# A VectorE loop over four pairs in place of eight, rings of four slots, and the edge mask made beside the scores

## The chip, the cores and the metric

The kernel runs on one core of a Trainium2 chip. Its engines are PE (TensorE), VectorE (DVE), ScalarE (ACT), GpSimd (POOL) and SyncE (SP), each with an instruction stream of its own; they meet by semaphores. The metric is the device time of one execution in microseconds (us), the median of several runs.

## The reference

Four graph layers over 6,250 nodes of 128 features and 200,000 edges follow one another, each on a normalised and rectified copy `h` of the nodes and each added to them: a sum over neighbours with two linear layers, a filter convolution, an attention layer (GATv2), and the relation layer. The change touches the last alone:

```python
def relation(entity_emb, rel_embed_weight, W, heads, rels, tails):
    e_h, e_t, e_r = entity_emb[heads], entity_emb[tails], rel_embed_weight[rels]
    score = jnp.sum(e_t * jnp.tanh(e_h + e_r), axis=-1)
    score_exp = jnp.exp(score - jnp.max(score))
    score_sum = segment_sum(score_exp, heads, n)
    attn = score_exp / (score_sum[heads] + 1e-10)
    agg = segment_sum(attn[:, None] * e_t, heads, n)
    return leaky_relu((entity_emb + agg) @ W.T, 0.2)
x = x + relation(h, rel, W, src, edge_type_64, dst)
```

## The kernel before

The layers run one after the other. For the relation layer the edges lie sorted by `src`, in groups of 512 (`GE`, four columns of 128 edges: `KG` = 4). Nodes lie in windows of 128. A *pair* is a group and a window that it has edges in; 392 groups are loaded and 440 pairs (`NG`) are worked through, in the order of lists that the chip has made itself (`k.plan`). An edge of the group that belongs to another window is a foreign edge of the pair.

A pair goes through these steps, all in `relation`:
- SyncE loads the group's records (`rows`, L2251); GpSimd gathers its 512 target rows with four indirect DMAs (`far`, L2278) into a ring of eight slots, and waits on `rows_free` for a free one (SyncE's L2265).
- `columns` (VectorE, L2297 to 2299): each edge's place in the window (`rel`), its type (`kind`), and the mask `hide`, a large negative number for foreign edges.
- `spread_keys` (PE, L2405) and `take_keys` (ScalarE, L2360) bring place and type into rows; `one_hots` (VectorE, L2306, L2307) compares them into `hot_t` and `kind_t`.
- `near` (PE, L2417 to 2420) fetches `e_h + e_r` with matmuls over these, `terms` (ScalarE, L2365) takes the tanh.
- `score_edges` (VectorE): four products with a sum (`work`, L2318), the mask added (`score`, L2324), the group's highest per partition (`peak`, L2327).
- `spreads` (PE, L2435), `running_max` (VectorE, L2334 `before`, L2336 `gmax`, L2339 `cur`), `exps` (ScalarE, L2371, L2373).
- `turn_hot` (PE, L2428), `share_out` (ScalarE, L2382), `sums` (PE, L2444), `add` (VectorE, L2347: the running row, `cur`), `keep` (ScalarE, L2391).

Each engine runs a hardware loop (`skewed`) whose body works through several pairs (`turn`) and holds the steps in the order of the call. A step with lead 7 (`COLS`) works seven pairs ahead of one with lead 0 (`ADD`), so in one pass of VectorE the add is for pair n, the scores for n+3, the one-hots for n+5, the columns for n+7. At the head of `columns` and of `score_edges` the engine reads the number of the pair's group from the lists into a register (`pair_group`, L1230); records and gathered rows are then addressed by it. VectorE's, ScalarE's and PE's loops here take eight pairs (`S` = 2 x `U` = 8); the loop's end is L1206. `wait(..., behind)` waits until a step is done for the pair that lies `behind` before, which guards a ring of that many slots.

Of the kernel before, what the change touches and what calls it, by code (L numbers as in the profile page):

```python
# [18 lines left out]
P = 128  # L19
# [2184 lines left out]
def relation(k):  # L2204
# [15 lines left out]
    with ExitStack() as own:  # L2220
        sb = lambda name, shape, dt=F32: k.sb(own, "r_" + name, shape, dt)
        rows, keys = sb("rows", [P, R, KG, MW - M_SRC], I32), sb("keys", [P, 2, 2, GE], BF16)
        rel, hide, kind = sb("rel", [P, S, KG]), sb("hide", [P, S, KG]), sb("kind", [P, S, KG])
        hot_t, kind_t = sb("hot_t", [P, H, GE], BF16), sb("kind_t", [P, U, GE], BF16)
        far = sb("far", [P, S, KG, XW])
        work, raw, score, peak = sb("work", [P, KG, D]), sb("raw", [P, KG]), sb("score", [P, S, KG]), sb("peak", [P, S])
        gmax, before, factor = sb("gmax", [P, 1]), sb("before", [P, S]), sb("factor", [P, S])
        prob, share = sb("prob", [P, S, KG]), k.store[:, 10 * NL:10 * NL + 2 * GE].rearrange("p (b q c) -> p b q c", b=2, q=KG)
# [15 lines left out]
        with nc.Block() as block:  # L2244
# [39 lines left out]
            @block.vector  # L2284
            def _(dve):
                now = Counts(dve)
                k.link(dve, nc.vector.memset(cur[:, :, :], 0.0))
                k.link(dve, nc.vector.memset(cur[:, :, D + 1:D + 2], -LOW))
                k.link(dve, nc.vector.memset(far[:, :, :, D:XW], 1.0))
                start(dve, cols_ready, onehotT_ready, edge_dot, masked, scores, group_max, exp_in, added)  # L2290

                def columns(g, a):
                    u, f = a % S, bass.ds(g + a, 1)
                    group = pair_group(dve, k, o, g + a)
                    dve.wait_ge(records_in, in_order(group))
                    row = lambda c: flat(rows[:, bass.ds(slot_of(group, R), 1), :, c - M_SRC])
                    nc.vector.tensor_scalar(rel[:, u, :], row(M_SRC), base[:, f], None, ALU.subtract)  # L2297
                    nc.vector.tensor_copy(kind[:, u, :], row(M_TYPE)).then_inc(cols_ready, 1)
                    nc.vector.tensor_scalar(hide[:, u, :], row(M_BASE), base[:, f], -BIG, ALU.not_equal, ALU.mult)

                def one_hots(g, a):
                    h, b = a % H, a % 2
                    wait(dve, now, keys_taken, g, a)
                    wait(dve, now, onehot_turned, g, a, H)
                    wait(dve, now, near_ready, g, a, U)
                    nc.vector.tensor_scalar(hot_t[:, h, :], keys[:, b, 0, :], k.part_id[:, 0:1], None, ALU.is_equal)  # L2306
                    nc.vector.tensor_scalar(kind_t[:, a % U, :], keys[:, b, 1, :], k.part_id[:, 1:2], None, ALU.is_equal)\  # L2307
                        .then_inc(onehotT_ready, 1)

                def score_edges(g, a):  # L2310
                    u, b = a % S, a % 2
                    group = pair_group(dve, k, o, g + a)
                    slot = bass.ds(slot_of(group), 1)
                    dve.wait_ge(rows_here, in_order(group))
                    wait(dve, now, edge_term, g, a)
                    wait(dve, now, scores, g, a, 1)
                    for q in range(KG):
                        last = nc.vector.scalar_tensor_tensor(  # L2318
                            work[:, q, :], near_ps[b][:, q * D:(q + 1) * D], 1.0, flat(far[:, slot, q, 0:D]), ALU.mult, ALU.mult,
                            accum_out=raw[:, q:q + 1])  # L2320
                    last.then_inc(edge_dot, 1)
                    wait(dve, now, edge_dot, g, a)
                    wait(dve, now, weighed, g, a, S)
                    nc.vector.tensor_tensor(score[:, u, :], raw[:, :], hide[:, u, :], ALU.add).then_inc(masked, 1)  # L2324
                    wait(dve, now, masked, g, a)
                    wait(dve, now, spread, g, a, S)
                    nc.vector.tensor_reduce(peak[:, u:u + 1], score[:, u, :], AX, ALU.max).then_inc(scores, 1)  # L2327

                def running_max(g, a):
                    u, f = a % S, bass.ds(g + a, 1)  # L2330
                    past = cur[:, (u - 1) % S, D + 1:D + 2]
                    wait(dve, now, exp_in, g, a, 1)
                    wait(dve, now, shrink, g, a, S)
# [3 lines left out]
                    wait(dve, now, kept, g, a, S)  # L2337
                    wait(dve, now, group_max, g, a)
                    nc.vector.scalar_tensor_tensor(cur[:, u, D + 1:D + 2], gmax[:, :], -1.0, past, ALU.mult, ALU.min)\  # L2339
                        .then_inc(exp_in, 1)  # L2340

                def add(g, a):
                    u, b = a % S, a % 2
# [3 lines left out]
                    nc.vector.scalar_tensor_tensor(cur[:, u, 0:D + 1], cur[:, (u - 1) % S, 0:D + 1], factor[:, u:u + 1],  # L2347
                                                   sum_ps[b][:, 0:D + 1], ALU.mult, ALU.add).then_inc(added, 1)
                skewed(dve, (HOT, one_hots), (ADD, add), (SCORE, score_edges), (MAX, running_max), (COLS, columns),
                       counts=now, turn=S)  # L2350

            @block.scalar
            def _(act):
# [11 lines left out]
                    nc.scalar.activation(near_ps[b], near_ps[b], ACT.Tanh).then_inc(edge_term, 1)  # L2365

                def exps(g, a):
                    u = a % S
                    wait(act, now, exp_in, g, a)
                    wait(act, now, prob_ready, g, a, S)  # L2370
                    nc.scalar.activation(prob[:, u, :], score[:, u, :], ACT.Exp, bias=cur[:, u, D + 1:D + 2]).then_inc(weighed, 1)  # L2371
                    wait(act, now, added, g, a, S)
                    nc.scalar.activation(factor[:, u:u + 1], before[:, u:u + 1], ACT.Exp, scale=-1.0,  # L2373
                                         bias=cur[:, u, D + 1:D + 2]).then_inc(shrink, 1)

                def share_out(g, a):
                    u, b = a % S, a % 2
                    wait(act, now, weighed, g, a)
                    wait(act, now, onehot_turned, g, a)
                    wait(act, now, summed, g, a, 2)  # L2380
                    for q in range(KG):
                        last = nc.scalar.activation(share[:, b, q, :], hot_ps[:, q * P:(q + 1) * P], ACT.Copy, scale=prob[:, u, q:q + 1])  # L2382
                    last.then_inc(prob_ready, 1)

                def keep(g, a):
                    wait(act, now, added, g, a)
                    act.sem_inc(k.loading, 1)
                    wait(act, now, kept, g, a, 1)
                    act.sem_inc(k.loading, 1)
                    w = pair_window(act, k, o, g + a)  # L2390
                    nc.scalar.activation(k.acc[:, w, 0:D + 2], cur[:, a % S, 0:D + 2].unsqueeze(1), ACT.Copy).then_inc(kept, 1)  # L2391
                skewed(act, (WEIGH, share_out), (KEYS, take_keys), (NEAR, terms), (MAX, exps), (ADD, keep), counts=now, turn=S)

            @block.tensor
            def _(pe):
# [1 line left out]
                start(pe, keys_spread, near_ready, onehot_turned, spread, summed)  # L2397

                def spread_keys(g, a):
                    u = a % S  # L2400
# [28 lines left out]
                    last.then_inc(onehot_turned, 1)  # L2429

                def spreads(g, a):
                    u = a % S
# [312 lines left out]
```

## Time and profile before

| | |
|---|---|
| median of 3 runs | 9282.66 us (9282.63 to 9282.89) |
| the profiled execution | 9295.66 us, its span 9294.0 us |
| busy over the span | PE 7420.9 us (80%), VectorE 6266.4 (67%), GpSimd 6250.4 (67%), ScalarE 5033.5 (54%) |
| the relation stage | from about 7103 us, when it clears its running rows, to 9250 us, its last add |

The profile is of one execution. A row of the timeline has an instruction's start, its length, engine, line, operation and operands (written <- read); in brackets stands how long the engine's data path was idle before it and what ended that. "issue" means nothing that the profile shows. Waits, register arithmetic, loads of registers and jumps are done by the engine's sequencer; they are not counted as busy and stand under the name DVEq. A wait's releaser is inferred.

### The profile page before, as it was taken

What the parts mean: (1) busy time and instruction counts of PE and PEld (TensorE: products, weight loads), DVE (VectorE), ACT (ScalarE), POOL (GpSimd) and SP (SyncE); (2) the same over time, 40 slices, a digit from 0 to 9 for tenths busy, and PEclk for the clock granted to TensorE, in tenths of its full rate; (3) what the DMA queues carried; (4) which work ended last, traced back from release to release, by engine and by line L of the source; (5) the groups of instructions that cost most, each with busy time, mean ns of one, the idle gap of its engine ahead of it and who ended that gap; (6) DMA issues with size and microseconds to landing.
All of it is one profiled execution on the core that took longest, in us unless ns stands there. A gap on an engine that the chain in (4) does not pass through costs nothing. (4 is left out here: it accounts for less than half of the span.)

```text
span 9294.0 us, 257139 instructions
## 1 busy us (share of the span) xinstructions
PE 7420.9 (80%) x48775; PEld 5025.9 (54%) x49109; DVE 6266.4 (67%) x20821; ACT 5033.5 (54%) x11808; POOL 6250.4 (67%) x6542
## 2 busy tenths in 40 slices
PE   3699999996666666666978999999995777777777
PEld 2344455554333333335965666666663666666666
DVE  6577777776444455557976777777777666666666
ACT  4366666664333333332334555666665666666666
POOL 4777777772777777774217777777763766766664
PEclk7555555557888888888989999999998999999999
DMA  6355555553333344446842222222221222222221
GB/s 191 103 143 144 147 148 150 150 150 98 107 109 110 113 113 116 115 117 189 262 124 55 56 55 55 54 53 54 52 45 38 54 51 51 51 51 50 51 51 48
DMA packets 1004337, 900.19 MB, mean 97 GB/s; under 512 B 689602, under 2 KB 748099, under 8 KB 1003590
## 3 DMA queue, kind: packets, MB, share of 16 engines
q0 software_dynamic: 243504, 526.87, 21.2%
q10 hardware_dynamic: 309878, 260.87, 9.9%
q1 hardware_dynamic: 450592, 109.24, 5.4%
q14 instruction: 334, 2.74, 0.1%
q8 instruction: 29, 0.48, 0.0%
HBM read 663.38 MB, written 248.90 MB: 98 GB/s over the span
## 5 line engine op out<-in xcount | busy, mean ns | idle before, releaser
L2022 POOL DMA_INDIRECT a_far<-attention_table,a_rows x1568 | 1548.2, 987 | 657.9 <-issue 489.2
L1769 POOL DMA_INDIRECT message_records<-hs,f_pos x1564 | 1522.1, 973 | 622.9 <-issue 438.2
L2278 POOL DMA_INDIRECT r_far<-node_table,r_rows x1568 | 1488.7, 949 | 636.1 <-issue 452.2
L1377 POOL DMA_INDIRECT near<-split_table,t_rows x1568 | 1518.4, 968 | 482.1 <-issue 476.9
L1859 ACT ACTIVATE hs<-banks,f_rows 128x128 f32 x1760 | 503.1, 368 | 1200.6 <-DVE hs L1819 1084.5
L1565 PE MATMUL banks<-near,w_f 20*128 20x512 f32 x784 | 807.6, 1130 | 26.5 <-DVE list_store L1453 25.1
L1556 PE MATMUL banks<-near,t_hot 128*128 x5292 | 694.8, 304 | 167.0 <-SPq L1352 106.9
L1556 PEld LDWEIGHTS banks<-near,t_hot 128*128 128x128 bf16 x5292 | 586.1, 135 | 313.0 <-issue 228.3
L2129 ACT ACTIVATE list_store<-banks,staging 128x512 f32<-128x512 f32 x442 | 303.9, 688 | 819.6 <-DVE staging L2086 817.6
L1900 PE MATMUL banks<-f_hot_t,near 128*128 128x512 bf16 x1218 | 420.4, 458 | 357.3 <-DVE f_hot_t L1797 348.1
L1818 DVE COPY hs<-f_rows 128x12 int32 x441 | 84.7, 192 | 887.7 <-SPq L1753 884.6
L2417 PE MATMUL banks<-near,r_hot_t 128*128 x5328 | 621.7, 232 | 39.2 <-issue 1.9
L2194 PEld LDWEIGHTS banks<-a_far,a_prob 128*128 128x128 f32 x3528 | 431.1, 190 | 276.6 <-issue 276.6
L1904 PE MATMUL banks<-list_store,w_W_f 128*128 128x512 f32 x886 | 559.2, 719 | 0.0
L1890 PEld LDWEIGHTS banks<-ident_b,f_rel 128*128 128x128 bf16 x1780 | 131.4, 107 | 754.2 <-DVE f_rel L1791 648.2
L1462 DVE SCALAR_TENSOR_TENSOR near<-list_store,xs 128x512 f32<-128x512 f32 x392 | 268.3, 684 | 394.3 <-ACT xs L1514 374.4
L2444 PE MATMUL banks<-r_far,list_store 128*128 x3528 | 531.6, 296 | 0.0
L2382 ACT ACTIVATE list_store<-banks,r_prob 128x128 f32<-128x128 bf16 x1764 | 498.3, 364 | 40.0 <-PE banks L2428 27.3
L1573 PEld LDWEIGHTS banks<-ident,t_attr 128*20 128x20 f32 x1568 | 156.0, 120 | 642.2 <-issue 587.2
L2417 PEld LDWEIGHTS banks<-near,r_hot_t 128*128 128x128 bf16 x5328 | 432.2, 103 | 120.9 <-issue 98.3
L1679 PE MATMUL banks<-m_rows,m_hot 128*128 128x128 f32 x3528 | 434.9, 281 | 65.5 <-DVE m_hot L1640 45.6
L2194 PE MATMUL banks<-a_far,a_prob 128*128 x3528 | 476.3, 277 | 8.9 <-issue 3.9
(445 smaller groups left out, 19688.3 us busy)
## 6 DMA issues: line engine op xcount, KB each, us to landing
list_store<-soft_groups ACTq DMA_DIRECT2D x447, 256.0 KB
soft_groups<-near ACTq DMA_DIRECT2D x392, 256.0 KB
m_rows<-message_records SPq DMA_DIRECT2D x223, 264.0 KB
m_rows<-message_records POOLq DMA_DIRECT2D x223, 264.0 KB
near<-split_table,t_rows POOLq DMA_INDIRECT x1568
a_far<-attention_table,a_rows POOLq DMA_INDIRECT x1568
r_far<-node_table,r_rows POOLq DMA_INDIRECT x1568
message_records<-hs,f_pos POOLq DMA_INDIRECT x1564
```

The lines of the kernel that those rows point to most:

```text
L1377: pool.indirect_dma_start(far[:, u * KG + q, :], None, k.table3[:, :], bass.IndirectOffsetOnAxis(ap=rows[:, u, q, C_SRC:C_SRC + 1].bitcast ...
L1556: last = nc.tensor.matmul(k.psum[a % 2][:, 0:D], hot[:, a % H, q, :], row[:, part * D:(part + 1) * D], start=q == 0 and part == 0, stop=q ...
L1565: nc.tensor.matmul(hidden_ps[a % 2], k.w_f1[:, :], attr_t[:, a % 2, :], start=True, stop=True).then_inc(hidden_ready, 1)
L1769: pool.indirect_dma_start(k.mrec[:, :], bass.IndirectOffsetOnAxis(ap=pos[:, u, q:q + 1], axis=0), msg[:, u * KG + q, :], None)\
L1859: last = nc.scalar.activation(msg[:, bass.ds(slot + q, 1), 0:D].rearrange("p a d -> p (a d)"), out_ps[b][:, q * D:(q + 1) * D], ACT.Copy, ...
L1904: nc.tensor.matmul(filter_ps[b], w_f2[:, :], soft[:, s, :], start=True, stop=True).then_inc(filter_ready, 1)
L2022: pool.indirect_dma_start(far[:, u, q, :], None, k.gtable[:, :], bass.IndirectOffsetOnAxis(ap=rows[:, a % R, q, C_SRC:C_SRC + 1].bitcast(I ...
L2194: last = nc.tensor.matmul(sum_ps[b][:, 0:D + 1], prob[:, b, q * P:(q + 1) * P], flat(far[:, slot, q, 0:D + 1]), start=q == 0, stop=q == KG ...
L2278: pool.indirect_dma_start(far[:, u, q, 0:D], None, k.table[:, :], bass.IndirectOffsetOnAxis(ap=rows[:, a % R, q, M_DST - M_SRC:M_DST - M_S ...
L2382: last = nc.scalar.activation(share[:, b, q, :], hot_ps[:, q * P:(q + 1) * P], ACT.Copy, scale=prob[:, u, q:q + 1])
L2417: nc.tensor.matmul(near_ps[b][:, span], hot_t[:, h, span], k.near[:, w, part * D:(part + 1) * D] .rearrange("p a d -> p (a d)"), start=par ...
L2444: last = nc.tensor.matmul(sum_ps[b][:, 0:D + 1], share[:, b, q, :], flat(far[:, slot, q, 0:D + 1]), start=q == 0, stop=q == KG - 1)
```

## The change

In `relation`, VectorE's loop takes four pairs a turn. Its steps stand in another order: add, scores, one-hots, maximum, columns, where the one-hots came first. The rings of `rel`, `kind`, `score`, `peak`, `before`, `factor`, `prob`, `cur` and `hot_t` have four slots in place of eight, so each wait that guards one looks four pairs back. The mask `hide` has one slot and is made in `score_edges`, not in `columns`, after a wait for the previous pair's masked score. ScalarE and PE keep their loops over eight pairs, their order and their instructions. The diff, cut (left out are the same replacement of `S` by `U` for the rings in `running_max`, `add`, ScalarE's and PE's steps, and the declaration of `prob`):

```diff
@@ -2207 +2207 @@ relation
-    S, H, R = 2 * U, 2 * U, 4 * U
+    S, H, R = 2 * U, U, 4 * U
@@ -2223 +2223 @@
-        rel, hide, kind = sb("rel", [P, S, KG]), sb("hide", [P, S, KG]), sb("kind", [P, S, KG])
+        rel, hide, kind = sb("rel", [P, U, KG]), sb("hide", [P, KG]), sb("kind", [P, U, KG])
...
-        work, raw, score, peak = sb("work", [P, KG, D]), sb("raw", [P, KG]), sb("score", [P, S, KG]), sb("peak", [P, S])
-        gmax, before, factor = sb("gmax", [P, 1]), sb("before", [P, S]), sb("factor", [P, S])
+        work, raw, score, peak = sb("work", [P, KG, D]), sb("raw", [P, KG]), sb("score", [P, U, KG]), sb("peak", [P, U])
+        gmax, before, factor = sb("gmax", [P, 1]), sb("before", [P, U]), sb("factor", [P, U])
...
-        cur = sb("cur", [P, S, XW])
+        cur = sb("cur", [P, U, XW])
@@ -2292 +2292 @@ vector: columns
-                    u, f = a % S, bass.ds(g + a, 1)
+                    u, f = a % U, bass.ds(g + a, 1)
...
                     nc.vector.tensor_copy(kind[:, u, :], row(M_TYPE)).then_inc(cols_ready, 1)
-                    nc.vector.tensor_scalar(hide[:, u, :], row(M_BASE), base[:, f], -BIG, ALU.not_equal, ALU.mult)
@@ -2310 +2309 @@ vector: score_edges
-                    u, b = a % S, a % 2
+                    u, b = a % U, a % 2
...
                     dve.wait_ge(rows_here, in_order(group))
+                    wait(dve, now, masked, g, a, 1)
+                    nc.vector.tensor_scalar(hide[:, :], flat(rows[:, bass.ds(slot_of(group, R), 1), :, M_BASE - M_SRC]), base[:, bass.ds(g + a, 1)],
+                                            -BIG, ALU.not_equal, ALU.mult)
                     wait(dve, now, edge_term, g, a)
...
-                    wait(dve, now, weighed, g, a, S)
-                    nc.vector.tensor_tensor(score[:, u, :], raw[:, :], hide[:, u, :], ALU.add).then_inc(masked, 1)
+                    wait(dve, now, weighed, g, a, U)
+                    nc.vector.tensor_tensor(score[:, u, :], raw[:, :], hide[:, :], ALU.add).then_inc(masked, 1)
                     wait(dve, now, masked, g, a)
-                    wait(dve, now, spread, g, a, S)
+                    wait(dve, now, spread, g, a, U)
@@ -2349 +2351 @@ vector: the loop
-                skewed(dve, (HOT, one_hots), (ADD, add), (SCORE, score_edges), (MAX, running_max), (COLS, columns),
-                       counts=now, turn=S)
+                skewed(dve, (ADD, add), (SCORE, score_edges), (HOT, one_hots), (MAX, running_max), (COLS, columns),
+                       counts=now, turn=U)
```

VectorE's instructions in the relation loop, one pair, from the end of its columns to the first product, before. The rows of L1230 read the group's number, REGISTER_ALU and ISA are work of the sequencer:

```order
L1162 REGISTER_ALU [waits keys_taken]
L2306 TENSOR_SCALAR r_hot_t<-r_keys,part_id 128x512 [waits near_ready,onehot_turned]
L2307 TENSOR_SCALAR r_kind_t<-r_keys,part_id 128x512
L2347 SCALAR_TENSOR_TENSOR r_cur<-r_cur,r_factor,banks 128x129 [waits added,shrink,summed]
L1230 ISA
L1230 TENSOR_LOAD list_store
L2314 REGISTER_ALU
L2318 REGISTER_ALU [waits scores,edge_term,rows_here]
L2318 REGISTER_ALU
L2318 ISA
L2318 SCALAR_TENSOR_TENSOR r_work,r_raw<-banks,r_far 128x128
```

And with the change, from the pair's add (which now follows the columns at once) to the wait before the first product; two register rows and the product follow:

```order
L2349 SCALAR_TENSOR_TENSOR r_cur<-r_cur,r_factor,banks 128x129 [waits added,shrink,summed]
L1230 ISA
L1230 TENSOR_LOAD list_store
L2313 REGISTER_ALU
L2315 REGISTER_ALU [waits masked,rows_here]
L2315 REGISTER_ALU
L2315 ISA
L2315 REGISTER_ALU
L2315 TENSOR_SCALAR r_hide<-r_rows,list_store 128x4
L2320 REGISTER_ALU [waits scores,edge_term]
L2320 REGISTER_ALU
```

The one-hots no longer stand between columns and add, and the mask with its own register row stands behind the load.

VectorE in the same pair, from the masked score to the running maximum, before:

```order
L2324 TENSOR_TENSOR r_score<-r_raw,r_hide 128x4 [waits weighed,edge_dot]
L2327 TENSOR_REDUCE r_peak<-r_score 128x1 [waits spread,masked]
L2334 ISA [waits shrink,exp_in]
L2334 TENSOR_SCALAR r_before<-r_cur,list_store 128x1
L2336 TENSOR_REDUCE r_gmax<-banks 128x1 [waits spread]
L2339 SCALAR_TENSOR_TENSOR r_cur<-r_gmax,r_cur 128x1 [waits group_max,kept]
```

With the change:

```order
L2326 TENSOR_TENSOR r_score<-r_raw,r_hide 128x4 [waits weighed,edge_dot]
L2329 TENSOR_REDUCE r_peak<-r_score 128x1 [waits spread,masked]
L2305 TENSOR_SCALAR r_hot_t<-r_keys,part_id 128x512 [waits near_ready,onehot_turned,keys_taken]
L2306 TENSOR_SCALAR r_kind_t<-r_keys,part_id 128x512
L2336 ISA [waits shrink,exp_in]
L2336 TENSOR_SCALAR r_before<-r_cur,list_store 128x1
L2338 TENSOR_REDUCE r_gmax<-banks 128x1 [waits spread]
L2341 SCALAR_TENSOR_TENSOR r_cur<-r_gmax,r_cur 128x1 [waits group_max,kept]
```

The two one-hots now stand between the peak and `before`. From the VectorE loop's head to its jump the listing has 278 rows before and 154 with the change; the attention stage's VectorE loop, over eight pairs, has 190. A pair has 35 to 37 of these rows in both.

## Rows read from the trace of the kernel before

**Rows 1.** Windows view of the relation stage; busy us (instructions) of each engine.
```profile
core 0: us, PE busy (x) PEld busy (x) DVE busy (x) ACT busy (x) POOL busy (x), PEclk, DMA share, GB/s
7160.00:9230.00 2070.00, 1617.31 (x17953) 1425.12 (x17951) 1355.76 (x8120) 1416.22 (x3845) 1446.65 (x1524) 0.93 0.24 51
```

**Rows 2.** Waits in 7160 to 9230: who waited for whom, us, times, longest.
```profile
POOL r_far L2278 <- issue: 440.0, 1387, 2.6
ACT r_prob L2371 <- DVE r_cur L2339: 358.6, 326, 5.1
...
PE banks L2405 <- DVE r_kind L2298: 219.0, 369, 1.0
...
DVE r_hot_t L2306 <- PE banks L2428: 187.7, 49, 4.2
POOL r_far L2278 <- SPq L2265: 169.0, 137, 5.2
```

**Rows 3.** Lines 2347 and 2278: min/median/max ns of one, first and last start.
```profile
L2347 DVE SCALAR_TENSOR_TENSOR r_cur<-r_cur,r_factor,banks x440: 329/340/351, 7125.2 to 9249.7; 128x129 f32<-128x129 f32 x147
L2278 POOL DMA_INDIRECT r_far<-node_table,r_rows x1568: 941/947/1074, 7104.6 to 9214.4; - x196
```

**Rows 4.** VectorE's timeline around one jump back: start, us, instruction, idle before.
```profile
7627.04 0.23 DVE L2299 TENSOR_SCALAR r_hide<-r_rows,list_store 128x4 f32 x1
7631.22 0.42 DVE L2306 TENSOR_SCALAR r_hot_t<-r_keys,part_id 128x512 bf16<-128x512 bf16 x1 [3.95 <-PE banks L2428]
```

**Rows 5.** The jump back (line 1206) of VectorE's relation loop, and what follows it.
```profile
L1206 DVEq COMPARE_BRANCH  x54: 62/63/78, 7163.1 to 9215.2; - x54
L1206 DVEq FUSED_REGOPS  x54: 51/51/51, 7166.9 to 9218.6; - x54
```

**Rows 6.** The same of VectorE's attention loop.
```profile
L1206 DVEq COMPARE_BRANCH  x54: 56/56/74, 4962.1 to 6959.0; - x54
L1206 DVEq FUSED_REGOPS  x54: 51/51/58, 4962.4 to 6959.2; - x54
```

**Rows 7.** DMA view, 7600 to 8000: instruction packets, MB, share.
```profile
q14 instruction: 51, 0.42, 0.4%
```

**Rows 8.** VectorE's timeline, one pair from its columns to the next pair's.
```profile
7639.52 0.24 DVE L2297 TENSOR_SCALAR r_rel<-r_rows,list_store 128x4 f32 x1 [0.70 <-issue]
...
7639.78 0.23 DVE L2299 TENSOR_SCALAR r_hide<-r_rows,list_store 128x4 f32 x1
7639.93 0.35 DVE L2306 TENSOR_SCALAR r_hot_t<-r_keys,part_id 128x512 bf16<-128x512 bf16 x1
7640.19 0.35 DVE L2307 TENSOR_SCALAR r_kind_t<-r_keys,part_id 128x512 bf16<-128x512 bf16 x1
7640.46 0.34 DVE L2347 SCALAR_TENSOR_TENSOR r_cur<-r_cur,r_factor,banks 128x129 f32<-128x129 f32 x1
7641.38 0.29 DVE L2318 SCALAR_TENSOR_TENSOR r_work<-banks,r_far 128x128 f32<-128x128 f32 x1 [0.58 <-issue]
...
7642.54 0.16 DVE L2327 TENSOR_REDUCE r_peak<-r_score 128x1 f32<-128x4 f32 x1
7642.74 0.21 DVE L2334 TENSOR_SCALAR r_before<-r_cur,list_store 128x1 f32<-128x1 f32 x1
...
7643.26 0.16 DVE L2339 SCALAR_TENSOR_TENSOR r_cur<-r_gmax,r_cur 128x1 f32<-128x1 f32 x1
7644.12 0.23 DVE L2297 TENSOR_SCALAR r_rel<-r_rows,list_store 128x4 f32 x1 [0.70 <-issue]
```

**Rows 9.** VectorE's timeline, another pair.
```profile
8004.59 0.23 DVE L2297 TENSOR_SCALAR r_rel<-r_rows,list_store 128x4 f32 x1 [0.70 <-issue]
...
8005.98 0.29 DVE L2318 SCALAR_TENSOR_TENSOR r_work<-banks,r_far 128x128 f32<-128x128 f32 x1
...
8008.75 0.39 DVE L2297 TENSOR_SCALAR r_rel<-r_rows,list_store 128x4 f32 x1 [0.70 <-issue]
```

**Rows 10.** The load of a register from the lists (line 1230) on VectorE's sequencer.
```profile
L1230 DVEq TENSOR_LOAD <-list_store x854: 299/308/327, 7161.7 to 9228.3; - x171
```

More of the change, by code:

```diff
@@ L2222, in relation @@
         rows, keys = sb("rows", [P, R, KG, MW - M_SRC], I32), sb("keys", [P, 2, 2, GE], BF16)
-        rel, hide, kind = sb("rel", [P, S, KG]), sb("hide", [P, S, KG]), sb("kind", [P, S, KG])
+        rel, hide, kind = sb("rel", [P, U, KG]), sb("hide", [P, KG]), sb("kind", [P, U, KG])
         hot_t, kind_t = sb("hot_t", [P, H, GE], BF16), sb("kind_t", [P, U, GE], BF16)
         far = sb("far", [P, S, KG, XW])
-        work, raw, score, peak = sb("work", [P, KG, D]), sb("raw", [P, KG]), sb("score", [P, S, KG]), sb("peak", [P, S])
-        gmax, before, factor = sb("gmax", [P, 1]), sb("before", [P, S]), sb("factor", [P, S])
-        prob, share = sb("prob", [P, S, KG]), k.store[:, 10 * NL:10 * NL + 2 * GE].rearrange("p (b q c) -> p b q c", b=2, q=KG)
-        cur = sb("cur", [P, S, XW])
+        work, raw, score, peak = sb("work", [P, KG, D]), sb("raw", [P, KG]), sb("score", [P, U, KG]), sb("peak", [P, U])
+        gmax, before, factor = sb("gmax", [P, 1]), sb("before", [P, U]), sb("factor", [P, U])
+        prob, share = sb("prob", [P, U, KG]), k.store[:, 10 * NL:10 * NL + 2 * GE].rearrange("p (b q c) -> p b q c", b=2, q=KG)
+        cur = sb("cur", [P, U, XW])
         loads_in, gathered = k.loads_in, k.gathered
@@ L2322, in score_edges @@
                     wait(dve, now, edge_dot, g, a)
-                    wait(dve, now, weighed, g, a, S)
-                    nc.vector.tensor_tensor(score[:, u, :], raw[:, :], hide[:, u, :], ALU.add).then_inc(masked, 1)
+                    wait(dve, now, weighed, g, a, U)
+                    nc.vector.tensor_tensor(score[:, u, :], raw[:, :], hide[:, :], ALU.add).then_inc(masked, 1)
                     wait(dve, now, masked, g, a)
-                    wait(dve, now, spread, g, a, S)
+                    wait(dve, now, spread, g, a, U)
                     nc.vector.tensor_reduce(peak[:, u:u + 1], score[:, u, :], AX, ALU.max).then_inc(scores, 1)
                 def running_max(g, a):
-                    u, f = a % S, bass.ds(g + a, 1)
-                    past = cur[:, (u - 1) % S, D + 1:D + 2]
+                    u, f = a % U, bass.ds(g + a, 1)
+                    past = cur[:, (u - 1) % U, D + 1:D + 2]
                     wait(dve, now, exp_in, g, a, 1)
-                    wait(dve, now, shrink, g, a, S)
+                    wait(dve, now, shrink, g, a, U)
                     nc.vector.tensor_scalar(before[:, u:u + 1], past, fresh[:, f], None, ALU.add)
@@ L2336, in running_max @@
                     nc.vector.tensor_reduce(gmax[:, :], peak_ps[:, 0:P], AX, ALU.max).then_inc(group_max, 1)
-                    wait(dve, now, kept, g, a, S)
+                    wait(dve, now, kept, g, a, U)
                     wait(dve, now, group_max, g, a)
@@ L2342, in add @@
                 def add(g, a):
-                    u, b = a % S, a % 2
+                    u, b = a % U, a % 2
                     wait(dve, now, summed, g, a)
@@ L2346, in add @@
                     wait(dve, now, added, g, a, 1)
-                    nc.vector.scalar_tensor_tensor(cur[:, u, 0:D + 1], cur[:, (u - 1) % S, 0:D + 1], factor[:, u:u + 1],
+                    nc.vector.scalar_tensor_tensor(cur[:, u, 0:D + 1], cur[:, (u - 1) % U, 0:D + 1], factor[:, u:u + 1],
                                                    sum_ps[b][:, 0:D + 1], ALU.mult, ALU.add).then_inc(added, 1)
-                skewed(dve, (HOT, one_hots), (ADD, add), (SCORE, score_edges), (MAX, running_max), (COLS, columns),
-                       counts=now, turn=S)
+                skewed(dve, (ADD, add), (SCORE, score_edges), (HOT, one_hots), (MAX, running_max), (COLS, columns),
+                       counts=now, turn=U)
             @block.scalar
@@ L2367, in exps @@
                 def exps(g, a):
-                    u = a % S
+                    u = a % U
                     wait(act, now, exp_in, g, a)
-                    wait(act, now, prob_ready, g, a, S)
+                    wait(act, now, prob_ready, g, a, U)
                     nc.scalar.activation(prob[:, u, :], score[:, u, :], ACT.Exp, bias=cur[:, u, D + 1:D + 2]).then_inc(weighed, 1)
-                    wait(act, now, added, g, a, S)
+                    wait(act, now, added, g, a, U)
                     nc.scalar.activation(factor[:, u:u + 1], before[:, u:u + 1], ACT.Exp, scale=-1.0,
@@ L2376, in share_out @@
                 def share_out(g, a):
-                    u, b = a % S, a % 2
+                    u, b = a % U, a % 2
                     wait(act, now, weighed, g, a)
@@ L2390, in keep @@
                     w = pair_window(act, k, o, g + a)
-                    nc.scalar.activation(k.acc[:, w, 0:D + 2], cur[:, a % S, 0:D + 2].unsqueeze(1), ACT.Copy).then_inc(kept, 1)
+                    nc.scalar.activation(k.acc[:, w, 0:D + 2], cur[:, a % U, 0:D + 2].unsqueeze(1), ACT.Copy).then_inc(kept, 1)
                 skewed(act, (WEIGH, share_out), (KEYS, take_keys), (NEAR, terms), (MAX, exps), (ADD, keep), counts=now, turn=S)
@@ L2399, in spread_keys @@
                 def spread_keys(g, a):
-                    u = a % S
+                    u = a % U
                     wait(pe, now, cols_ready, g, a)
@@ L2431, in spreads @@
                 def spreads(g, a):
-                    u = a % S
+                    u = a % U
                     wait(pe, now, scores, g, a)
```

## The prediction

> **What bounds the kernel now.** The change touches one stage, the relation layer, so I read that stage alone: its stretch of the windows view, its waits, then single pairs on VectorE's timeline. The stage's adds into the running row, one a pair, start at 7125.2 us and 9249.7 us, and there are 440 [rows 3]: (9249.7 - 7125.2) / 439 = 4.84 us a pair. In the stretch no engine is near full: VectorE is busy 1355.76 of 2070 us, PE 1617.31, GpSimd 1446.65 [rows 1]. The waits tell who leads. ScalarE waits for VectorE's running maximum, PE for VectorE's columns and maximum, GpSimd's gathers for free slots (169.0 us), that is for a compute side that is late [rows 2]. VectorE itself waits for others almost nowhere but in one place, 49 times before the one-hots (187.7 us), charged to PE [rows 2]. So VectorE's own stream paces the stage, and busy shares hide it, because much of its time is instruction issue.
>
> That one place is not PE. On the timeline the mask of a pair starts at 7627.04 us and the next VectorE instruction, the one-hot, at 7631.22, 4.18 us later [rows 4]; in an ordinary pair the same two lie 0.15 us apart (7639.78 to 7639.93) [rows 8]. Between them stands the loop's jump back: 54 of them, the first at 7163.1 us with the first instruction behind it at 7166.9, the last at 9215.2 and 9218.6 [rows 5]: 3.8 and 3.4 us. The attention stage's VectorE loop, also over eight pairs, has 4962.1 and 4962.4, 6959.0 and 6959.2 [rows 6]: 0.3 us. The relation stage is also the one where instruction packets flow while the loops run, 51 in 400 us [rows 7], five for each of the ten turns. So the relation loop's jump stalls on its code. In the order listing that loop has 278 rows from head to jump, the attention loop 190.
>
> Away from the jump a pair takes 4.16 us (8004.59 to 8008.75) [rows 9] or 4.60 (7639.52 to 7644.12) [rows 8]. Check: a turn of eight is 8 x 4.84 = 38.7 us; less the jump's 4.18 - 0.15 = 4.03 that leaves 34.7, or 4.33 a pair, between the two.
>
> **Term 1, the jump's stall goes: -218 us, of which 58 stay.** The new loop has 154 listing rows, fewer than the 190 that jump without a stall [rows 6], so I take all of 54 x 4.03 us away. The Trainium skill (Runtime: NRT & Kernel Launch, Instruction fetch mechanics) says that code comes in 16 KiB blocks, that two are held, and that a taken branch outside them waits for a transfer. By that the new jump is free too; the trace agrees that size decides, but its instruction packets are 8 KB each (0.42 MB in 51) [rows 7]. What stays is the ordinary jump: 4.03 less the 3.5 us by which these jumps (3.8) exceed the attention loop's (0.3), 0.53 us, now once in four pairs: 110 x 0.53 = **+58 us**, or 0.13 us a pair.
>
> **Term 2, the two one-hots move behind the scores: about +0.49 us a pair.** They were in the piece from the columns to the first product and now stand between peak and maximum. There peak to `before` is 7642.54 to 7642.74, 0.20 us [rows 8]. Now it is 0.15 to the one-hot (as mask to one-hot before), then 0.26 and 0.27 (their own spacings, 7639.93 to 7640.19 to 7640.46) [rows 8]: 0.69 us.
>
> **Term 3, the columns-to-product piece does not shrink for it.** The one-hots were not free time there: they covered a register load. VectorE's sequencer reads the pair's group from memory, 0.308 us each, twice a pair [rows 10], plus register arithmetic and waits at some 0.1 us a step. Before, the load stood behind hot, kind_t and add, over 0.7 us of queued work. In the 4.16 us pair it is mostly hidden: columns to first product 1.39 us (4.59 to 5.98) [rows 9]. In the 4.60 pair the add was late and the chain ran bare: add 7640.46, product 7641.38, 0.92 us (the load's 0.31 and six steps of 0.1), and 7639.52 to 7641.38 is 1.86 us [rows 8]. Now only kind and add stand ahead of it, as the listings of the change show, so it is always bare, and longer, because the mask with its own address sits in it:
> - rel to kind 0.13 (half of rel to mask, 7639.52 to 7639.78) [rows 8]; kind to add 0.15, as mask to one-hot.
> - add to mask: the same chain as cur to rel (load, three register operations, address, instruction), 7643.26 to 7644.12 = 0.86 us [rows 8], and one register operation more: 0.95.
> - mask to product: two register operations, an address and a wait, four steps of 0.1: 0.4. (Bare, the 0.92 chain plus a mask slot of 0.13 would give 1.05 in place of 0.95 + 0.4; that is the low end.)
>
> Together 1.63 us against 1.39 or 1.86: nothing gained over the mean. The mask itself leaves the columns (a slot of 0.13), which is why it is in this sum once only.
>
> **The sum, per pair:** 1.63 (rel to product) + 1.16 (product to peak, 7641.38 to 7642.54) + 0.69 + 0.52 (before to cur, 7642.74 to 7643.26) + 0.86 (cur to rel) [rows 8] = 4.86, plus 0.13 for the jump = 4.99. Rows 8 show an undisturbed pair; in others single instructions take longer (a one-hot 0.42 us against 0.35 [rows 4, 8], a rel 0.39 against 0.24 [rows 8, 9]). I take 0.06 us for that: **5.05 us a pair against 4.84**. 439 x 0.21 = **+92 us**.
>
> **What costs nothing, and why.** The rings of four: each new wait looks four pairs back at work that other engines do one or two pairs after it became possible, since they wait for VectorE [rows 2]. The tightest is the one-hot ring: the one-hot of pair n+5 now waits for PE's turning of pair n+1, the last thing PE does in a pair's step. PE is done with it before VectorE's columns release its next keys (PE waits 219.0 us for those [rows 2]), and the one-hot now comes some 3 us behind the columns, so the wait is covered; were PE later than that, the difference would be paid in every pair. The wait of the mask for the previous masked score is VectorE's own instruction, one pair old. The add comes sooner behind the columns than it did (the one-hots stood between), but the sums that it waits for are released by columns one pair older, so a pair of 5 us gives PE more time for them than before. The gathers: 1568, from 7104.6 to 9214.4 us [rows 3], with 169.0 us of waiting for slots [rows 2]; a slower compute side only lengthens that.
>
> **Rivals.**
> *Gathers become the bound (faster).* If the sequencer hides the load as in the 4.16 pair, the stall's loss wins. GpSimd then runs without its 169.0 us of slot waits, of which 137 x 0.3 is the gap that every gather has (440.0 us in 1387 [rows 2]): 128 us sooner, the last gather at 9086 us, and some 25 us behind it (five pairs and the landing) the last add, at 9111 instead of 9249.7: 9144 us. It decides below 4.45 us a pair: a gather and its gap are 0.947 + 0.3 us, a group's four 5.0, and there are 392 groups for 440 pairs. For it: 54 stalls are the only thing in this stage that looks like waste. Against: the bare 0.92 chain [rows 8] shows what happens when nothing is queued ahead. The halfway case, add to product 1.1 instead of 1.35, is 4.80 a pair: 9265 us. Chance of faster in any of these ways 0.15.
> *Nothing to measure.* Stall saved and load exposed are nearly equal: 5.05 would have to be 4.84, the 0.2 of my product chain too long. 9283 us, chance 0.07.
> *The stall stays and comes twice as often.* If the window that code is held in is not the reason for rows 6, 110 jumps stall for 3.5 us in place of 54: a pair takes 5.05 + 3.5/4 = 5.93 us, and 439 x 1.09 us more is 9760 us. Chance 0.04: a loop of 190 rows jumps freely, this one has 154.
> *A ring of four is too short.* VectorE waits for PE's turning or keys each pair, at 5.3 us or more: from 9485 us. Chance 0.04.
>
> **How the numbers follow.** The profiled execution took 9295.66 us with a span of 9294.0; the median of the runs is 9282.66, 13 us less. The sum is a difference in that execution and I add it to the median: 9282.66 + 92 = **9375 us**. My forecast has 0.70. Its own range is 4.88 to 5.2 us a pair, 9300 to 9445. The range 9255 to 9455 also takes in no change and the halfway case. A measurement of this kernel can tell about 0.2%, 19 us, from nothing. Faster 0.15, same 0.07, slower 0.78.
>
> **What would show it.** Right: jumps back 0.3 us long and twice as many; no instruction packets in the stage; first product some 1.3 us behind the add in every pair, with idle time charged to issue before the mask in the scoring step; adds 5.05 us apart; slot waits of the gathers well over 169 us. Wrong: pairs of 4.5 us with GpSimd gathering without pause; or idle time before the one-hots that ends with PE; or jumps still of 3.5 us.

## The result and the profile after

| | before | changed |
|---|---|---|
| median | 9282.65 us | 9366.97 us |
| ratio, with its 95% interval | | 1.0091 (1.0079 to 1.0104) |
| the profiled execution's span | 9294.0 us | 9367.3 us |
| adds of the relation stage, first to last | 7125.2 to 9249.7 us | 7114.9 to 9322.8 us |
| a pair, first to last add over 439 | 4.84 us | 5.03 us |

The change costs 84 us, 0.9%. In the stage itself it is 2207.9 - 2124.5 = 83.4 us; the span grew by 10 us less because the stages ahead were 10 us shorter in this one execution. The adds after, which answer to [rows 3]:

```profile
L2349 DVE SCALAR_TENSOR_TENSOR r_cur<-r_cur,r_factor,banks x440: 340/350/353, 7114.9 to 9322.8; 128x129 f32<-128x129 f32 x147
```

The jump back and what follows it, which answer to [rows 5]: twice as many, the first at 7176.0 us with the next instruction at 7176.3.

```profile
L1206 DVEq COMPARE_BRANCH  x108: 50/56/56, 7176.0 to 9327.5; - x108
L1206 DVEq FUSED_REGOPS  x107: 51/51/51, 7176.3 to 9307.9; - x107
```

The instruction packets of the whole execution, from the profile's part on DMA queues; before there were 334 of them with 2.74 MB, and between 7600 and 8000 us, where [rows 7] has 51, there is none now:

```profile
q14 instruction: 63, 0.52, 0.0%
```

VectorE's timeline of one pair, which answers to [rows 8]:

```profile
7643.72 0.32 DVE L2297 TENSOR_SCALAR r_rel<-r_rows,list_store 128x4 f32 x1 [0.69 <-issue]
7643.86 0.19 DVE L2298 CAST r_kind<-r_rows 128x4 f32 x1
7643.99 0.35 DVE L2349 SCALAR_TENSOR_TENSOR r_cur<-r_cur,r_factor,banks 128x129 f32<-128x129 f32 x1
7645.00 0.29 DVE L2315 TENSOR_SCALAR r_hide<-r_rows,list_store 128x4 f32 x1 [0.66 <-issue]
7645.36 0.29 DVE L2320 SCALAR_TENSOR_TENSOR r_work<-banks,r_far 128x128 f32<-128x128 f32 x1
...
7646.52 0.16 DVE L2329 TENSOR_REDUCE r_peak<-r_score 128x1 f32<-128x4 f32 x1
7646.64 0.35 DVE L2305 TENSOR_SCALAR r_hot_t<-r_keys,part_id 128x512 bf16<-128x512 bf16 x1
7646.91 0.35 DVE L2306 TENSOR_SCALAR r_kind_t<-r_keys,part_id 128x512 bf16<-128x512 bf16 x1
7647.18 0.21 DVE L2336 TENSOR_SCALAR r_before<-r_cur,list_store 128x1 f32<-128x1 f32 x1
...
7647.69 0.16 DVE L2341 SCALAR_TENSOR_TENSOR r_cur<-r_gmax,r_cur 128x1 f32<-128x1 f32 x1
7648.55 0.23 DVE L2297 TENSOR_SCALAR r_rel<-r_rows,list_store 128x4 f32 x1 [0.70 <-issue]
```

The add at 7643.99 us has only the kind ahead of it. Behind it the data path is idle for 0.66 us, charged to "issue": the sequencer reads the group's number and does its register arithmetic, and the mask comes 1.01 us after the add, the first product 0.36 later. The one-hots run after the peak. The pair takes 7648.55 - 7643.72 = 4.83 us; one in four has the jump between kind and add and takes some 0.55 more. Over all pairs of the stage the mask starts 0.99 us behind the add in the mean.

The waits in 7160 to 9320, which answer to [rows 2]: those of the gathers for slots rose from 169.0 to 213.8 us, and 254.0 us of idle time before VectorE's mask are new. The wait of the one-hots for PE is gone from the list.

```profile
ACT r_prob L2373 <- DVE r_cur L2341: 467.1, 413, 1.7
...
PE banks L2407 <- DVE r_kind L2298: 301.6, 389, 1.0
DVE r_hide L2315 <- issue: 254.0, 395, 0.7
POOL r_far L2278 <- SPq L2265: 213.8, 86, 5.6
```

### The profile page after: what moved, and what is told of

Same layout as the page of the kernel before. It is cut to its first block and busy times, and to the rows that moved or that the text cites. A ratio compares the mean times of both kernels' runs of the same rounds, so it can differ in the third digit from the quotient of the medians.

```text
span 9367.3 us, 258955 instructions
## 1 busy us (share of the span) xinstructions
PE 7436.2 (79%) x48775; PEld 4992.7 (53%) x49109; DVE 6307.4 (67%) x20817; ACT 5040.5 (54%) x11808; POOL 6229.8 (67%) x6542
```

## The experiments

Each time below is also put on one scale: its ratio to the kernel before, as run on the same chip, times 9282.65 us. A ratio's interval is 0.0010 to 0.0017 to either side, so a difference of two times on the scale is uncertain by 13 to 22 us. "New" is the change's order; "scores" and "columns" say which step makes the mask.

| kernel | pairs a turn | order | mask | rings | on the scale, us |
|---|---|---|---|---|---|
| before | 8 | one-hots first | columns | 8 | 9283 |
| x8_rings_but_hot | 8 | one-hots first | columns | 4, one-hots 8 | 9295 |
| x7_rings | 8 | one-hots first | columns | 4 | 9312 |
| x5_order | 8 | new | columns | 8 | 9404 |
| x6_turn8 | 8 | new | scores | 4 | 9479 |
| the change | 4 | new | scores | 4 | 9367 |
| x4_mask_cols | 4 | new | columns | 4 | 9232 |
| x1_hots_between | 4 | one-hots between add and scores | scores | 4 | 9241 |
| x3_old_order_mask_scores | 4 | one-hots first | scores | 4 | 9241 |
| x2_old_order | 4 | one-hots first | columns | 4 | 9124 |
| y1_hint | 8, jump hinted | one-hots first | columns | 8 | 9120 |
| y3_turn8_hint | 8, jump hinted | new | scores | 4 | 9297 |
| y2_kept | 4, one load fewer | new | scores | 4 | 9251 |

**The rings alone.**

```diff
-    S, H, R = 2 * U, 2 * U, 4 * U
+    S, H, R = 2 * U, U, 4 * U
...
-                    u, f = a % S, bass.ds(g + a, 1)
+                    u, f = a % U, bass.ds(g + a, 1)
```

> The kernel before with the rings of four slots alone (rel, hide, kind, score, peak, before, factor, prob, cur, hot_t); VectorE's loop stays at eight pairs, one-hots first, mask in the columns. Theory (the pace is VectorE's own stream; a jump's stall traded for an uncovered register load): no change, 9283 us within 19, pairs 4.84 us apart, 54 jumps of 3.5 us or more. Rival (rings of four make VectorE wait for PE or ScalarE): slower, with idle time before the one-hots in every pair; all of the +84 us if the rings are its cause, 9367.

Measured: 9316.70 us, ratio 1.0032 (1.0020 to 1.0043), 30 us slower. A small miss: I had expected nothing. The timeline of this run's VectorE, two pairs behind a jump's stall (the one-hot at 7596.40 was the first instruction after it):

```profile
7604.82 0.23 DVE L2299 TENSOR_SCALAR r_hide<-r_rows,list_store 128x4 f32 x1
7606.21 0.35 DVE L2306 TENSOR_SCALAR r_hot_t<-r_keys,part_id 128x512 bf16<-128x512 bf16 x1 [1.17 <-PE banks L2428]
```

The one-hot waits 1.17 us for PE's turning. The reading: that is the ring of four for the one-hots, and it bites here because PE is late behind a stall, and four slots leave less room than eight to make up for it. The waits view of this run has 90 waits of the one-hots for PE, 231.9 us, against 49 and 187.7 us [rows 2]. The next run gives the one-hots their eight slots back:

```diff
-    S, H, R = 2 * U, U, 4 * U
+    S, H, R = 2 * U, 2 * U, 4 * U
```

> The run with the rings of four alone, but with eight slots for the one-hots. There two pairs behind each jump the adds were 5.4 to 5.5 us apart in about half of the turns (4.2 to 4.4 before), with idle time of VectorE before the one-hots that ended with PE's turning. Theory: that is the wait of the one-hot ring alone, which bites only behind the jump's stall, when PE is late: with eight slots 9283 us again. Rival (other rings, or the code's place in memory, make the 30 us): 9313 us.

Measured: 9311.43 us beside 9298.97, ratio 1.0013 (1.0003 to 1.0022). On the scale the one-hot ring makes 18 of the 30 us, give or take 14. The traces say it more sharply: the third add behind a jump comes 4.24 us after the second in the kernel before, 4.94 with all rings of four, and 4.29 with eight slots for the one-hots (means of 54 turns). The other 12 us are at the edge of what can be told and were not pursued.

**The order alone.**

```diff
-                skewed(dve, (HOT, one_hots), (ADD, add), (SCORE, score_edges), (MAX, running_max), (COLS, columns),
+                skewed(dve, (ADD, add), (SCORE, score_edges), (HOT, one_hots), (MAX, running_max), (COLS, columns),
                        counts=now, turn=S)
```

> The kernel before with the new order of VectorE's steps alone (add, scores, one-hots, maximum, columns); eight pairs a turn, rings of eight, mask in the columns. Theory: the register load loses its cover, add to first product goes to 0.92 us in every pair (columns to product 1.37 instead of 1.54 in the mean), peak to `before` from 0.20 to 0.69, and the jump still stalls: about 0.3 us a pair more, 9283 + 439 x 0.3 = 9415 us (9385 to 9445). Rival (order does nothing, instructions only change places): 9283 us.

Measured: 9408.74 us, ratio 1.0131 (1.0114 to 1.0148), so +121 us where +132 was expected. The order by itself costs more than the whole change.

**The turn alone, from the change's side.**

```diff
-                       counts=now, turn=U)
+                       counts=now, turn=S)
```

> The changed kernel with VectorE's loop at eight pairs again, all else as changed. Theory: the stall of the jump comes back, 54 jumps of 3.5 us more, and 54 ordinary jumps of 0.53 us go: 9367 + 189 - 29 = 9527 us (9500 to 9550), instruction packets in the stage again. Rival (the stall was nothing that the loop's size sets, or it was covered by other waits): 9367 us or a little less.

Measured: 9483.94 us, ratio 1.0212 (1.0195 to 1.0229), +112 us to the changed kernel where +160 was expected: a miss. The stall is back, and so are the instruction packets (334 in the execution). The jump itself is shorter in this body: jump and next instruction are 2.8 us apart at either end and 2.90 in the mean, against 3.8 and 3.4 [rows 5] and a mean of 3.68.

```profile
L1206 DVEq COMPARE_BRANCH  x54: 62/63/78, 7152.5 to 9392.8; - x54
L1206 DVEq FUSED_REGOPS  x54: 51/51/51, 7155.3 to 9395.6; - x54
```

54 x (2.8 - 0.3) = 135, less the 29 for jumps saved, is 106, close to the 112. That closeness is luck. The run with the hint, y3_turn8_hint below, shows that the stall costs this body 182 us, near the 189 expected, and that a body of eight wins 47 us elsewhere that the expectation did not have.

**Four pairs and rings of four, old order and mask.**

```diff
-                skewed(dve, (ADD, add), (SCORE, score_edges), (HOT, one_hots), (MAX, running_max), (COLS, columns),
+                skewed(dve, (HOT, one_hots), (ADD, add), (SCORE, score_edges), (MAX, running_max), (COLS, columns),
                        counts=now, turn=U)
```

(and the mask in `columns`, in a ring of four, as in the next run.)

> Loop of four pairs and rings of four as in the change, but the one-hots first and the mask in the columns as before: the change's gain without its cost. Theory: 4.33 us a pair + 0.13 for the jumps = 4.46, which is also the gathers' pace (5.0 us a group x 392 / 440): the gathers run nearly without slot waits, 9144 us (9115 to 9180). Rival (ring of four for the one-hots is too short where they come first, PE's turning is late): idle time before the one-hots that ends with PE, 4.7 us a pair or more, 9220 us or more.

Measured: 9129.33 us, ratio 0.9829 (0.9813 to 0.9846). The good part of the change is worth 159 us. Against x7_rings, from which only the turn differs, it is 188 us. The gathers set the pace now: they wait 4.9 us for slots in the whole stage, and run from 7098.7 to 9068.8 us, against 7104.6 to 9214.4 [rows 3].

```profile
L2278 POOL DMA_INDIRECT r_far<-node_table,r_rows x1568: 941/947/1077, 7098.7 to 9068.8; - x196
```

**The mask back in the columns, in the change.**

```diff
+                    nc.vector.tensor_scalar(hide[:, u, :], row(M_BASE), base[:, f], -BIG, ALU.not_equal, ALU.mult)
...
-                    wait(dve, now, masked, g, a, 1)
-                    nc.vector.tensor_scalar(hide[:, :], flat(rows[:, bass.ds(slot_of(group, R), 1), :, M_BASE - M_SRC]), base[:, bass.ds(g + a, 1)],
-                                            -BIG, ALU.not_equal, ALU.mult)
```

> The changed kernel with the mask made in the columns again (ring of four), all else as changed. Theory: in the profile of the changed kernel the mask and its addressing lie in the uncovered chain, add to mask 0.99 and mask to first product 0.36 us; without it the chain is the bare 0.90 that the run with the order alone has, and the columns get a slot of 0.13: 5.03 - 1.35 + 0.90 + 0.13 = 4.71 us a pair, 9367 - 439 x 0.32 = 9227 us (9205 to 9250). Rival (the place of the mask is indifferent, it is one instruction of 0.25 us in either): 9367 us.

Measured: 9247.67 us beside 9298.97, ratio 0.9945 (0.9929 to 0.9962): 9232 us on the scale, 135 less than the change, as expected. One instruction of 0.25 us costs 0.31 us a pair by its place: its slot, four register steps and the wait stand in a chain that nothing covers.

**The one-hots first, or between add and scores, with the mask in the scores.**

```diff
-                skewed(dve, (ADD, add), (SCORE, score_edges), (HOT, one_hots), (MAX, running_max), (COLS, columns),
+                skewed(dve, (ADD, add), (HOT, one_hots), (SCORE, score_edges), (MAX, running_max), (COLS, columns),
```

> The changed kernel with the one-hots first again, the mask still in the scoring step. Theory: one-hots cover a part of the load and of the mask's addressing; peak to `before` is back at 0.20 (minus 0.49 us), the load starts about 0.07 us later behind the columns: 5.03 - 0.42 = 4.61 us a pair, 9367 - 184 = 9183 us (9155 to 9215), above the 9129 of the run that has the mask in the columns too. Rival (the mask alone makes the difference, order nothing): 9367 us.

> The changed kernel with the one-hots between add and scores. Theory: what counts is that work is queued on VectorE ahead of the load, not that the one-hots are first: the same as the run with the one-hots first and the mask in the scores, 9183 us (9155 to 9215). Rival (the one-hots must come before the add, because PE or the sums wait for them): as the changed kernel, 9367 us, with new idle time before the add or the product.

Measured: 9256.97 and 9256.89 us, both 0.9955 (0.9938 to 0.9972): 9241 us. That the two agree was expected: what counts is work queued ahead of the load, not which step is first. The gain of 126 us in place of the 184 expected was a miss: the cover is partial. The timeline of the run with the one-hots between:

```profile
7643.27 0.35 DVE L2349 SCALAR_TENSOR_TENSOR r_cur<-r_cur,r_factor,banks 128x129 f32<-128x129 f32 x1
7643.53 0.35 DVE L2305 TENSOR_SCALAR r_hot_t<-r_keys,part_id 128x512 bf16<-128x512 bf16 x1
7643.79 0.35 DVE L2306 TENSOR_SCALAR r_kind_t<-r_keys,part_id 128x512 bf16<-128x512 bf16 x1
7644.44 0.23 DVE L2315 TENSOR_SCALAR r_hide<-r_rows,list_store 128x4 f32 x1 [0.30 <-issue]
7644.80 0.29 DVE L2320 SCALAR_TENSOR_TENSOR r_work<-banks,r_far 128x128 f32<-128x128 f32 x1
```

Add to mask is 1.17 us here with the one-hots in between (0.52 of it is their slots), against 1.01 in the change's pair. Over all pairs it is 1.21 against 0.99, and peak to `before` falls from 0.70 to 0.20: 439 x (0.50 - 0.22) = 123 us, which is the gain measured. The sequencer has to issue the one-hots and their wait before it comes to the load, and 0.30 us still lie open ahead of the mask.

**The stall by itself.** One instruction more in the kernel before, at the head of the loop, that announces the taken jump:

```diff
-    with eng.Fori(0, whole, turn) as g:
+    with eng.bass.Fori(0, whole, turn, engines=bass.OrderedEngineSet([eng.engine]), hint_back_edge=hint) as g:
...
-                       counts=now, turn=S)
+                       counts=now, turn=S, hint=True)
```

Measured: 9116.39 us, ratio 0.9825 (0.9809 to 0.9842). The 54 jumps of the same eight-pair body take 0.3 to 0.4 us with the hint, and the gathers wait 7.0 us for slots in the whole stage (169.0 [rows 2]):

```profile
L1206 DVEq COMPARE_BRANCH  x55: 55/61/105, 7145.6 to 9069.7; - x55
L1206 DVEq BRANCH_PREFETCH_HINT  x54: 47/47/47, 7145.9 to 9035.4; - x54
L1206 DVEq FUSED_REGOPS  x54: 51/51/51, 7146.0 to 9035.5; - x54
```

```profile
L2278 POOL DMA_INDIRECT r_far<-node_table,r_rows x1568: 940/944/1076, 7087.1 to 9051.8; - x196
...
  SPq L2265: 7.0, 23
```

The instruction packets of the whole execution fell with it, from 334 to the 63 that the change has too, and between 7600 and 8000 us there is none:

```profile
q14 instruction: 63, 0.52, 0.0%
```

So the idle time that the waits view charged to PE was a wait for the loop's own code. The Trainium skill says so of taken branches (Runtime: NRT & Kernel Launch, Instruction fetch mechanics): one whose target is outside the held pages waits for a fetch. The trace agrees in the wait, 3.22 to 4.19 us in the kernel before and 2.76 to 3.26 us in x6_turn8; no run here measures how much code is held.

The 271 packets that went are five for each of the 54 jumps. That the packets go, and not only their wait, was not expected: the expectation had the code fetched early. How the hint does it no run shows. The jumps gave back 54 x (3.68 - 0.35) = 180 us, the span of the stage's adds only 166: the gathers set the pace here as in x2_old_order, and between add and first product 45 us were added.

**The hint in the change with eight pairs.** The same edit, on x6_turn8.

> The changed kernel with VectorE's loop at eight pairs again (that run took 112 us more than the changed kernel) and the hint for its jump. Theory: the loop's length matters through the stall alone; with the hint 54 ordinary jumps fewer than in the changed kernel, at 0.53 us, less 54 hints of some 0.1 us: 9367 - 23 = 9344 us (9325 to 9365). Rival (a longer body costs by itself, or the stall is not the code): 9480 us.

Measured: 9294.74 us, ratio 1.0016 (1.0006 to 1.0026), 9297 us on the scale. Two things follow.

The stall costs the changed body at eight pairs 9479 - 9297 = 182 us, or 3.4 us a jump. That is more than the jumps themselves show: by the traces of the two runs 138 us of it lie between kind and add, where the jump stands, and 40 in three other places of the turn (rel to kind, product to peak, peak to one-hot). Why those grow was not tried.

And the kernel is 47 us better than expected, a miss: a body of eight differs from one of four by more than its jumps. The mask comes some 0.80 us behind the add in 218 of 439 pairs of this run and some 0.99 in the others, where the change has 0.99 in all but one. A pair with the short chain:

```profile
7644.27 0.35 DVE L2349 SCALAR_TENSOR_TENSOR r_cur<-r_cur,r_factor,banks 128x129 f32<-128x129 f32 x1
7645.06 0.23 DVE L2315 TENSOR_SCALAR r_hide<-r_rows,list_store 128x4 f32 x1 [0.45 <-issue]
```

In such a pair two steps of the sequencer are gone, the address step ahead of the load and a register step before the mask. Line 1230 of this run, in 7130 to 9420, has 651 address steps for 869 loads:

```profile
L1230 DVEq TENSOR_LOAD <-list_store x869: 298/306/322, 7133.3 to 9243.7; - x174
L1230 DVEq FUSED_REGOPS  x651: 57/57/65, 7133.2 to 9243.6; - x163
```

The other bodies of eight are alike: x6_turn8, without the hint, has 636 for 848 and the same short chain in 219 pairs, and the kernel before has 642 for its 854 loads. The change has 860 for 860. Between add and mask the trace of this run is 42 us shorter than the change's, and x6_turn8's is 41 us shorter, so the saving is there with and without the hint. Why a body of eight needs fewer steps was not tried.

**The load by itself.** The change, with the group's number kept in a register from the columns to the scores:

```diff
+                    nc.regs_mov(kept_group[u], group)
...
-                    group = pair_group(dve, k, o, g + a)
+                    group = nc.snap(kept_group[u], min_val=1, max_val=NGA)
```

> The changed kernel, but the scoring step takes the group's number from the register that the columns loaded four pairs before, so one load and its address step a pair are gone (2 of 37 instructions), nothing else. Theory: in the change this load stands uncovered, so all of it is gained: 0.31 + 0.03 for the load and 0.1 for the address step, 0.43 us a pair, add to mask 0.56 instead of 0.99: 9367 - 439 x 0.43 = 9178 us (9155 to 9210). Rival (the load runs beside other work and costs little): 9340 us or more.

Measured: 9248.63 us beside 9279.77, ratio 0.9966 (0.9954 to 0.9979): 116 us less than the change where 189 was expected. From the run's timeline:

```profile
7645.73 0.16 DVE L2344 SCALAR_TENSOR_TENSOR r_cur<-r_gmax,r_cur 128x1 f32<-128x1 f32 x1
7646.65 0.25 DVE L2300 TENSOR_SCALAR r_rel<-r_rows,list_store 128x4 f32 x1 [0.77 <-SPq L2257]
...
7647.48 0.35 DVE L2352 SCALAR_TENSOR_TENSOR r_cur<-r_cur,r_factor,banks 128x129 f32<-128x129 f32 x1 [0.53 <-issue]
7648.12 0.23 DVE L2318 TENSOR_SCALAR r_hide<-r_rows,list_store 128x4 f32 x1 [0.28 <-issue]
```

Add to mask is 0.64 us in place of 1.01, so 0.37 and not 0.43 came off, and cur to rel is 0.92 in place of 0.86: each chain has a register copy of some 0.07 in it. Over all pairs it is 0.63 against 0.99, and 0.95 against 0.86: 439 x (0.36 - 0.09) = 119, where 116 were measured. The load is exposed, and it is worth what its chain says.

## Why the prediction was right

Forecast 9375 us, measured 9367; +92 us in the stage, measured +83. The steps of the sum, from the one pair that is shown:

| step | forecast | measured |
|---|---|---|
| rel to kind, kind to add | 0.13, 0.15 | 0.14, 0.13 |
| add to mask | 0.95 | 1.01 |
| mask to first product | 0.4 | 0.36 |
| product to peak | 1.16 | 1.16 |
| peak to `before`, with the one-hots | 0.69 | 0.66 |
| `before` to cur, cur to rel | 0.52, 0.86 | 0.51, 0.86 |
| the ordinary jump, once in four pairs | 0.53 | about 0.55 |
| added for single instructions that take longer | 0.06 | 0.06 (what is left) |
| mean pair | 5.05 | 5.03 |

Each step of the sum came out within 0.06 us, so the number is no balance of errors. The 5.05 us are added up from the pieces of a pair without a stall; the stall's length enters only through the 4.84 us that were measured before and the 0.53 us left for an ordinary jump.

*Term 1, the stall.* Right: the stall is the loop's code, since the hint alone removes it together with its instruction packets (y1_hint), and 154 rows jump freely. The size is right too: the prediction took 3.5 us a jump for it; the 54 jumps before exceed the hinted ones by 3.68 - 0.35 = 3.3 us in the mean, and in the changed body at eight pairs the hint takes off 3.4 us a jump. What the prediction did not have is that a loop over eight pairs also spares the sequencer some steps that the loop over four has. Where the load is exposed this is worth 47 us (y3_turn8_hint against its expectation). The sum did not need it, since its add to mask counts every step.

*Term 2, the one-hots behind the peak.* Right, 0.66 against 0.69 (0.70 in the mean of all pairs).

*Term 3, the exposed load.* Right: 1.64 us from rel to product against 1.63, and shown from three sides: the order alone costs 121 us (x5_order), work put back ahead of the load gains 126 (x1, x3), the load taken out gains 116 (y2_kept). Taking x2_old_order as the base, the new order costs 9232 - 9124 = 108 us with the mask in the columns, and the mask's place 135 more on top; with the old order the mask's place costs 9241 - 9124 = 117. In x2_old_order the gathers set the pace (4.9 us of slot waits), which can hide part of either. The prediction also names a low end for this chain, 1.05 us from add to product; that would be 4.75 us a pair, below the 4.88 where its own range starts. The chain measured, 1.35 in the mean, is the one that the sum used.

*What costs nothing.* The rings of four: right for the change, whose waits view has no wait of the one-hots for PE. With the stall still there they cost 30 us (x7_rings), which I had not seen. In the change the stall that made PE late is gone. The slot waits of the gathers rose to 213.8 us, above the 169.0 as the prediction said, but hardly "well over".

*The rivals.* The gathers as the bound was the outcome of two other kernels, at 9124 and 9120 us, close to the 9144 worked out. It failed for the change because the load is not hidden there. "Ring too short" fell with the waits view, "stall twice as often" with the jumps at 0.3 us.

Two kernels of the study beat both: the kernel before with the one hinted jump (ratio 0.9825), and four pairs a turn with rings of four but the old order and mask (0.9829). They cannot be told from each other.

## What to carry to other kernels

An idle stretch of several us that returns once a turn, at the loop's head, may be the jump and not the engine that the waits view names, as it was here: look at the branch's row, at the next row of the sequencer and at the instruction packets before shortening a loop or lengthening a ring. To price such a stall, take it away and leave the body as it is: comparing two lengths of the loop also compares two bodies, and here the second difference hid 47 us of the first. Where a sequencer must load a register before an instruction, the order of the steps decides whether that load is hidden; in this kernel it needs work queued on the engine ahead of it that lasts as long as the load's chain, some 0.9 us, and an instruction moved behind the load brings its own register steps into the open.

## What the runs showed of the hardware

The stall of a jump is not a constant. From the branch to the sequencer's next instruction it is 3.22 to 4.19 us in one body, and 2.76 to 3.26 us in another with the same number of pairs and more instructions (388 against 363 records of VectorE and its sequencer in a turn). One hint instruction of 0.05 us at the loop's head brought it to 0.34 to 0.42 us in both, the length that it has in the bodies of four, and no instruction packets flowed between 7600 and 8000 us, where 51 and 48 did without it.

A load of a register from the lists takes 0.31 us, but with the steps around it it is a chain of some 0.9 us when nothing is queued on the engine ahead of it (add to first product in x4_mask_cols, 0.93 in the mean).
